# A four-layer graph stack on one core: one PE step split in two, and all engines' orders written anew

## The chip, the cores and the metric

The kernel runs on 1 core of one Trainium2 chip. Times are device microseconds of a whole launch, given as the median of several runs. The profiler adds one execution with every instruction's start and end.

## What is computed

Sixteen graphs of 1024 nodes with 128 features pass through four layers; each adds its result to its input and normalises over the features:

```python
x = _layernorm(x + _L0_gnn_ref(x, adj, W, a))            # one head, additive attention, relu
x = _layernorm(x + _L1_gnn_ref(x, adj, adj, W, a))       # 8 heads of 16, leaky scores, elu
x = _layernorm(x + _L2_gnn_ref(x, adj, rel_w, ...))      # mean over neighbours, linear, norm, relu
x = _layernorm(x + _L3_gnn_ref(x, adj, W))               # 4 heads of 32, dot-product attention
```

`adj` is a 0/1 matrix of 1024 x 1024 for each graph (int32 in memory, about 3% ones).

## The kernel before, in words

One graph is called a batch, b. All tiles of 128 nodes are T = 8. PE is TensorE, DVE VectorE, ACT ScalarE, POOL GpSimd, SP SyncE. Each engine runs one instruction stream, and the streams meet only at semaphores.

**The pipeline.** In a period, four batches are worked on at once: layer 0 and the start of layer 1 for batch n = f+1, the main part of layer 1 for f, layer 2 and layer 3 for k = f-1, and the end of layer 3 for m = f-2. `SECTIONS` lists the periods and `STAGE` says which table serves which: the first three periods have tables of their own (stages 0 to 2), thirteen full periods share one (stage 3), and the last batches have one (stage 4). A table is a dict of step numbers, one number (or list) for a named task, or -1 where the task isn't done; at each step every engine calls the tasks that have this number. So the tables `ON_PE`, `ON_ACT`, `ON_DVE`, `ON_POOL`, `ON_SP` are the order of the work, written out by hand or by a search; they add no wait of their own.

**The tasks that matter here.**

- Layer 0 of batch n: `turn0` (two halves, L895: four transposes each into the same PSUM bank, ACT copies each out to `xfT` before the next), `project0` (three parts, L907, the same bank again, ACT copies `st` and `features` after each), `top0`/`spread0` (L918, L922), `unit0` (eight units, L947: ACT makes a weight tile, L1274, DVE masks it, L1580, PE multiplies, 16 matmuls for one unit).
- Layer 1 of batch f: 64 units in 32 pairs `unit1`: ACT makes two ramps (L1330) from a row spread over all partitions (`s1row`, loaded by SP, L709), or DVE makes them itself (L1660); DVE cuts them with the adjacency (L1674), PE multiplies (L1022, 16 matmuls for a pair). After every four pairs DVE reduces the PSUM (`head1`, L1682). `sum1` (eight tasks, L1003, 24 matmuls each) multiplies the adjacency itself.
- Layer 2 of batch k: `self2` (L1050, L1055), `sum2` (L1069, L1072), and then `turn3`, `project3` (L864, L1088, L1094).
- Layer 3 of batch k: `lengths3`, `maxima3`, `shift3` make a bound for the exponent (DVE L1794 to L1810, PE L1099, L1103); `far` (SP, L754) moves half a tile across partitions by DMA; `scores3` (L1124 for masked ones, L1131), `exp3` (ACT L1378), `masked3` (DVE L1820), `values3` (L1148).
- End of layer 3 of batch m: `turn_back` (L1165): 32 transposes of 33 x 33, in two halves with a semaphore between them; then DVE `finish3` (L1835, L1839), POOL's `residual3`, `stats3`, `tail3`.

**The adjacency's way.** POOL `adjacency` (L831) copies one graph's matrix from int32 to bf16 in DRAM (2048 KB written). SP `adjacency` (L736) issues the DMA transpose into `turned`. POOL `narrow` (L820) copies that to fp8 in `AT`. SP `x` (L699) loads the features of batch n. SP `store_row` and `spread_row` (L717, L721) send a row of layer 0 to DRAM and back to all partitions; DVE `z0` (L1562) and ACT `prepare0` (L1248) wait for it.

The split task, as the kernel before has it, is one function with a wait between its halves:

```python
for x in range(2):
    if x:
        pe.wait_ge(first_turned.sem, first_turned.of(b))
    ...
    last.then_inc((sum3_turned if x else first_turned).sem, 1)
```

## Time and profile before

| | |
|---|---|
| median of 3 runs | 2420.53 us (2417.59 to 2421.40) |
| profiled execution, its own time | 2423.86 us |
| its span, first to last instruction | 2422.1 us |
| PE (matmul) busy | 2242.2 us, 93% |
| DVE busy | 1977.9 us, 82% |
| ACT busy | 1938.1 us, 80% |
| mean granted TensorE clock | 0.969 of full speed |
| DMA | 193.76 MB, 80 GB/s |

How to read it: an engine's busy time is the union of its instructions. Matmuls are pipelined, so a listed matmul is longer than the time that it adds to its group. A clock of 1.00 is 2.4 GHz, and a clock of 0.50 is 1.2 GHz; a stretch with both reads between. Idle time of an engine is put down to what ended it.

### The profile page before, as it was taken

The page shows a single profiled execution, that of the slowest core. Times are in us where ns is not written, and L with a number is a line of the kernel's source. Part 1 is how long each engine was busy: PE and PEld are TensorE (multiplying, and loading weights), DVE is VectorE, ACT ScalarE, POOL GpSimd, SP SyncE. Part 2 cuts the span into 40 slices and gives each one's busy share as a digit, 9 for nine tenths or more (in the row PEclk, how much of TensorE's full clock was granted, in tenths as well). Part 3 has the DMA queues.
Part 4 walks back from the last instruction along what each step waited for, and adds up shares of the span by engine and source line. Part 5 has one row for each costly group of instructions (what it writes and reads, how often), then busy time and mean ns, then how long its engine had stood idle before and what let it go on. Part 6 is the DMA issues. An engine that isn't in the chain of part 4 may idle for free.

```text
span 2422.1 us, 56777 instructions
## 1 busy us (share of the span) xinstructions
PE 2242.2 (93%) x23701; PEld 1528.8 (63%) x23701; DVE 1977.9 (82%) x4206; ACT 1938.1 (80%) x2166; POOL 192.2 (8%) x134
## 2 busy tenths in 40 slices
PE   6667999999999999999999999999999999999977
PEld 5567566585765748576575857658585665857442
DVE  4587788988888898888889888888888889888767
ACT  3858798797988879788787979879797987979735
POOL 0000000001000100100010000001000010010000
PEclk8888999999999999999999999999999999999998
DMA  5625016043251613416062251605225160411100
GB/s 92 159 59 125 19 63 140 28 107 70 70 132 54 141 36 97 80 63 140 29 148 54 69 108 63 140 28 130 63 63 123 61 142 28 106 36 65 34 19 18
DMA packets 190864, 193.76 MB, mean 80 GB/s; under 512 B 129368, under 2 KB 165328, under 8 KB 187728
## 3 DMA queue, kind: packets, MB, share of 16 engines
q1 hardware_dynamic: 183008, 132.99, 20.4%
q0 software_dynamic: 7600, 57.15, 12.1%
q8 instruction: 187, 3.06, 0.5%
q14 instruction: 69, 0.57, 0.1%
HBM read 151.26 MB, written 40.43 MB: 79 GB/s over the span
## 4 chain that ended last, share of the span: by engine, by line
PE 64%; ACT 13%; DVE 11%; issue 7%; DMA 5%; SPq 0%; POOL 0%; ACTq 0%; POOLq 0%; DVEq 0%
PE kp L1148 13%; PE kp L1131 10%; PE fp L1022 9%; PE kp L1003 6%; PE fp L947 6%; ACT ramp L1330 5%; ACT weight L1378 4%; PE kp L1072 4%; PE kp L1124 4%; DVE weight L1580 3%; DMA shared<-shared 2%; PE kp L1069 2%; DVE weight L1820 2%; PE fp L871 2%; PE kp L1165 1%
## 5 line engine op out<-in xcount | busy, mean ns | idle before, releaser
L1330 ACT ACTIVATE ramp<-s1row,tbig 128x1024 fp8e4<-128x1024 f32 x854 | 910.9, 1156 | 12.1 <-DMA s1row<-s_rows_dram 11.9
L1378 ACT ACTIVATE weight<-kp,shift 128x1024 f32<-128x1024 f32 x480 | 511.0, 1112 | 272.1 <-PE kp L1131 266.3
L1148 PE MATMUL kp<-weight,w 128*33 128x512 f32 x1920 | 447.4, 597 | 2.3 <-DVE weight L1820 1.3
L1022 PE MATMUL fp<-vh_parts,weight 128*128 128x102 bf16 x8192 | 418.1, 209 | 30.8 <-issue 11.2
L1022 PEld LDWEIGHTS fp<-vh_parts,weight 128*128 128x128 fp8e4 x8192 | 392.9, 98 | 79.9 <-issue 54.1
L1674 DVE TENSOR_TENSOR weight<-ramp,AT 128x512 int32<-128x512 int32 x512 | 341.7, 687 | 116.3 <-ACT ramp L1330 106.6
L1820 DVE SCALAR_TENSOR_TENSOR weight<-AT,weight 128x1024 f32<-128x1024 fp8e4 x272 | 319.8, 1219 | 46.9 <-ACT weight L1378 46.9
L1131 PE MATMUL kp<-shared 32*128 32x512 f32 x1920 | 274.1, 640 | 23.3 <-ACT weight L1378 23.2
L1148 PEld LDWEIGHTS kp<-weight,w 128*33 128x33 f32 x1920 | 96.7, 110 | 280.2 <-issue 247.9
L947 PEld LDWEIGHTS fp<-features,weight 128*128 128x128 f32 x1840 | 208.8, 192 | 41.1 <-issue 24.4
L1003 PE MATMUL kp<-vh_parts,AT 128*128 128x136 bf16 x3072 | 231.6, 239 | 0.0
L947 PE MATMUL fp<-features,weight 128*128 128x129 f32 x1840 | 217.4, 277 | 5.7 <-DVE weight L1580 5.7
L1003 PEld LDWEIGHTS kp<-vh_parts,AT 128*128 128x128 fp8e4 x3072 | 221.3, 103 | 0.8
L1682 DVE TENSOR_REDUCE vh<-fp 128x272 f32<-128x816 f32 x128 | 128.6, 1005 | 67.5 <-PE fp L1022 66.9
L1131 PEld LDWEIGHTS kp<-shared 32*128 32x128 f32 x1920 | 76.6, 183 | 148.2 <-issue 75.8
L1072 PE MATMUL kp<-elu,AT 128*128 128x128 bf16 x1920 | 170.1, 221 | 0.0
L1069 PE MATMUL kp<-y_hi,AT 128*128 128x129 bf16 x960 | 166.9, 222 | 3.1 <-DVE elu L1734 3.1
L1580 DVE SCALAR_TENSOR_TENSOR weight<-weight,v,AT 128x1024 f32<-128x1024 f32 x123 | 151.8, 1281 | 9.4 <-ACT weight L1274 8.6
L1274 ACT ACTIVATE weight<-xfT,v0neg,v0s 128x1024 f32<-128x1024 f32 x123 | 146.2, 1233 | 13.9 <-PE fp L947 11.9
L1072 PEld LDWEIGHTS kp<-elu,AT 128*128 128x128 fp8e4 x1920 | 149.7, 98 | 0.2
L1124 PE MATMUL kp<-AT,big 128*128 128x512 fp8e4 x480 | 128.0, 382 | 22.1 <-DMA shared<-shared 15.8
L797 POOL TENSOR_TENSOR bsmall<-bsmall,half_neg 128x8 f32<-128x8 f32 x32 | 65.8, 2055 | 878.7 <-DVE bsmall L1480 878.7
(251 smaller groups left out, 2729.8 us busy)
## 6 DMA issues: line engine op xcount, KB each, us to landing
s1row<-s_rows_dram SPq DMA_DIRECT2D x128, 512.0 KB, 4.7
adj_bf_dram<-in_adj_dram POOLq DMA_DIRECT2D x15, 2048.0 KB, 15.2
AT<-turned POOLq DMA_DIRECT2D x15, 1024.0 KB, 9.6
x<-in_x_dram SPq DMA_DIRECT2D x16, 512.0 KB, 6.7
out_dram<-elu SPq DMA_DIRECT2D x16, 512.0 KB, 10.4
xfT<-s_row_dram SPq DMA_DIRECT2D x15, 512.0 KB, 4.5
shared<-shared SPq DMA_DIRECT2D x30, 256.0 KB, 3.7
elu<-x POOLq DMA_DIRECT2D x15, 512.0 KB, 4.6
```

The source lines that it names most:

```text
L947: last = pe.matmul(sums0(b)[:, g, n * (D + 1):(n + 1) * (D + 1)], ring0(b, jt)[:, t * P:(t + 1) * P], h0[:, jt, :], start=(jt == 0 and n = ...
L1003: last = pe.matmul(kp[:, SUM_A_BANKS[t // PER], n * H1 * C1:(n + 1) * H1 * C1].rearrange("p (h c) -> p h c", h=H1), AT[:, third, jt, t * P ...
L1022: last = pe.matmul(fp[:, 1 + t // 4, col:col + 2 * PARTS * C1], edges[:, u % B_RING, t * P:(t + 1) * P], vh_parts[:, jt, h, :, :, :].rearr ...
L1072: last = pe.matmul(sums2(b)[:, g, col:col + D], lhsT, low2(b)[:, jt, k, :], start=False, stop=(jt == T - 1 and k == 1), skip_group_check=True)
L1124: pe.matmul(score_banks(b, w)[:, x, :], big[:], AT[:, third, 2 * J + x, n * HALF:(n + 1) * HALF], start=True, stop=False, skip_group_check ...
L1131: last = pe.matmul(score_banks(b, w)[:, x, :], mine[:, jt * P:(jt + 1) * P], mine[:, n * HALF:(n + 1) * HALF], start=v in masks(b), stop=True,
L1148: last = pe.matmul(kp[side(h), 0, :], values3(b)[:, (2 * J + x) * H3 + h, :], weight3[:, w % P_RING, x * HALF:(x + 1) * HALF], start=(J == ...
L1330: act.activation(ramp[:, u % R_RING, :], s1row[:, h % S_RING, :] if b or h else kp_pair, ACT.Relu, bias=tbig1[:, jt, h:h + 1], scale=BIG, ...
L1378: act.activation(weight3[:, w % P_RING, :], score_banks(b, w).rearrange("p a n -> p (a n)"), ACT.Exp, bias=shifts3(b)[:, h:h + 1], scale=R ...
L1580: dve.scalar_tensor_tensor(out=w, in0=w, scalar=v0[:, jt:jt + 1], in1=AT[:, third, jt, :], op0=ALU.add, op1=ALU.mult).then_inc(weight0_rea ...
L1674: dve.tensor_tensor(edge_words[:, u % B_RING:u % B_RING + 2, :], ramp_words[:, u % R_RING:u % R_RING + 2, :], AT_words[:, third, jt:jt + 2 ...
L1820: dve.scalar_tensor_tensor(out=mine, in0=AT[:, third, 2 * J:2 * J + 2, n * HALF:(n + 1) * HALF], scalar=0.0, in1=mine, op0=ALU.is_equal if ...
```

## The change

1. `layer3_turn_back` becomes two tasks, one for each half, each with a step number of its own. The second half's wait for the first stays. The 32 transposes are the same.
2. Every table has new step numbers, `STEPS` grows from 135 to 138. No table gains or loses any other task. Tiles, rings, semaphores and arithmetic are as before.

```diff
-        STEPS = 135
+        STEPS = 138
...
-            (dict(adjacency=1, narrow=-1, residual3=-1, rstd0=0, rstd1=-1, rstd2=-1, rstd3=-1, rstd_tail=-1),),
-            (dict(adjacency=0, narrow=1, residual3=-1, rstd0=2, rstd1=3, rstd2=-1, rstd3=-1, rstd_tail=-1),),
...
+            (dict(adjacency=0, narrow=-1, residual3=-1, rstd0=1, rstd1=-1, rstd2=-1, rstd3=-1, rstd_tail=-1),),
+            (dict(adjacency=2, narrow=0, residual3=-1, rstd0=1, rstd1=3, rstd2=-1, rstd3=-1, rstd_tail=-1),),
...
-            def layer3_turn_back(b, k):
-
-                pe.wait_ge(sum3_ready.sem, sum3_ready.of(b))
-                if k is not None and k < NB - 1:
-                    pe.wait_ge(sum2_read.sem, sum2_read.of(k))
-                for x in range(2):
-                    if x:
-                        pe.wait_ge(first_turned.sem, first_turned.of(b))
...
+            def layer3_turn_back(b, k, x):
+
+                if x:
+                    pe.wait_ge(first_turned.sem, first_turned.of(b))
+                else:
+                    pe.wait_ge(sum3_ready.sem, sum3_ready.of(b))
+                    if k is not None and k < NB - 1:
+                        pe.wait_ge(sum2_read.sem, sum2_read.of(k))
...
-                if m is not None and s == at["turn_back"]:
-                    layer3_turn_back(m, k)
+                for x in range(2):
+                    if m is not None and s == at["turn_back"][x]:
+                        layer3_turn_back(m, k, x)
```

**PE, a full period, around the turn back.** Before, both halves are one run of 32 (L1165) in the middle of `sum1` (L1003), and the two halves of `turn0` (L895) have other work between them:

```order
L1003 MATMUL kp<-vh_parts,AT 128x136 x48
L895 MATMUL fp<-ident,x 128x128 x4
L1003 MATMUL kp<-vh_parts,AT 128x136 x24
L895 MATMUL fp<-ident,x 128x128 x4
L1022 MATMUL fp<-vh_parts,weight 128x102 x16
L1003 MATMUL kp<-vh_parts,AT 128x136 x24
L1022 MATMUL fp<-vh_parts,weight 128x102 x16
L1165 MATMUL kp<-ident,shared 128x33 x32
L1003 MATMUL kp<-vh_parts,AT 128x136 x96
L1022 MATMUL fp<-vh_parts,weight 128x102 x16
L907 MATMUL fp<-rhs,xfT 128x130 x3
L1022 MATMUL fp<-vh_parts,weight 128x102 x16
```

The same place of the changed kernel:

```order
L1003 MATMUL kp<-vh_parts,AT 128x136 x48
L895 MATMUL fp<-ident,x 128x128 x8
L1022 MATMUL fp<-vh_parts,weight 128x102 x16
L1003 MATMUL kp<-vh_parts,AT 128x136 x24
L907 MATMUL fp<-rhs,xfT 128x130 x3
L1003 MATMUL kp<-vh_parts,AT 128x136 x24
L1165 MATMUL kp<-ident,shared 128x33 x16
L907 MATMUL fp<-rhs,xfT 128x130 x3
L1022 MATMUL fp<-vh_parts,weight 128x102 x16
L1165 MATMUL kp<-ident,shared 128x33 x16
L1003 MATMUL kp<-vh_parts,AT 128x136 x48
L1022 MATMUL fp<-vh_parts,weight 128x102 x16
```

The run of 32 is now two runs of 16 with a part of `project0` and a pair of layer 1 between them; the two halves of `turn0` follow each other directly.

**PE, a full period, at the units of layer 0** (L947, 8 matmuls a unit here), with scores (L1124, L1131) and values (L1148) of layer 3. Before:

```order
L947 MATMUL fp<-features,weight 128x129 x24
L1131 MATMUL kp<-shared 128x512 x4
L947 MATMUL fp<-features,weight 128x129 x16
L1148 MATMUL kp<-weight,w 33x512 x4
L947 MATMUL fp<-features,weight 128x129 x24
L1124 MATMUL kp<-AT,big 128x512 x4
L1131 MATMUL kp<-shared 128x512 x4
L1148 MATMUL kp<-weight,w 33x512 x4
L1131 MATMUL kp<-shared 128x512 x4
```

Now:

```order
L947 MATMUL fp<-features,weight 128x129 x24
L1131 MATMUL kp<-shared 128x512 x4
L947 MATMUL fp<-features,weight 128x129 x40
L1124 MATMUL kp<-AT,big 128x512 x4
L1131 MATMUL kp<-shared 128x512 x4
L1148 MATMUL kp<-weight,w 33x512 x8
L1131 MATMUL kp<-shared 128x512 x4
```

A pair of values (L1148) has moved from between the units to behind the next scores.

**POOL, the first three periods.** The adjacency load (L831), the copy to fp8 (L820) and the small powers of the norms (L797), with what was taken out and put in:

```order
+L831 DMA adj_bf_dram<-in_adj_dram 64x16384
 L797 TENSOR_TENSOR small<-small,half_neg 128x8
-L831 DMA adj_bf_dram<-in_adj_dram 64x16384 x2
 L820 DMA AT<-turned 128x8192
 L797 TENSOR_TENSOR small<-small,half_neg 128x8
+L831 DMA adj_bf_dram<-in_adj_dram 64x16384
 L797 TENSOR_TENSOR fsmall<-fsmall,half_neg 128x8
```

The load for batch 1 comes ahead of the first power, the load for batch 2 moves behind the power of batch 1's layer 0, and in the same way the load for batch 3 (one period on) moves behind that of batch 2's layer 0. On SP the DMA transpose now stands ahead of the load of x in the first periods, and in the full ones ahead of the last two row loads and of `far`, which it followed before.

## Rows read from the trace of the kernel before

**Rows 1.** The page: PE's busy time; granted clock in 40 slices, tenths.
```profile
PE 2242.2 (93%) x23701; PEld 1528.8 (63%) x23701; DVE 1977.9 (82%) x4206; ACT 1938.1 (80%) x2166; POOL 192.2 (8%) x134
...
PEclk8888999999999999999999999999999999999998
```

**Rows 2.** Two full periods: length, PE, PEld, DVE, ACT, POOL busy, PEclk, DMA share, GB/s.
```profile
1617.30:1759.70 142.40, 137.09 (x1481) 92.94 (x1479) 121.73 (x261) 120.82 (x136) 11.97 (x8) 1.00 0.35 87
1759.70:1903.20 143.50, 138.22 (x1481) 94.35 (x1479) 121.74 (x261) 120.62 (x136) 11.96 (x8) 0.99 0.36 86
```

**Rows 3.** The chain that ended last: start, length; one step of three periods.
```profile
904.29 5.28 PE kp L1148 x24
...
1046.35 5.28 PE kp L1148 x24
...
1189.87 5.28 PE kp L1148 x24
```

**Rows 4.** Stretches at and behind the turn back, in two periods (columns as Rows 2).
```profile
1081.26:1083.67 2.41, 2.35 (x35) 2.20 (x34) 2.34 (x6) 2.41 (x4) 0.00 (x0) 1.00 0.00 0
1083.67:1088.00 4.33, 4.33 (x46) 4.33 (x46) 4.26 (x11) 0.34 (x1) 0.00 (x0) 0.61 0.01 4
...
1655.91:1658.32 2.41, 2.35 (x35) 2.20 (x34) 2.34 (x6) 2.41 (x3) 0.00 (x0) 1.00 0.03 7
1658.32:1662.60 4.28, 4.28 (x68) 4.28 (x68) 4.21 (x11) 1.58 (x4) 0.00 (x0) 1.00 0.00 0
```

**Rows 5.** PE timeline right behind the turn back, in the same two periods.
```profile
1083.60 7.89 PE L1003 MATMUL kp<-vh_parts,AT 128*128 128x136 bf16 x96
...
1658.26 6.46 PE L1003 MATMUL kp<-vh_parts,AT 128*128 128x136 bf16 x96
```

**Rows 6.** PE, ACT and SP timeline of one full period, with PE's waits in brackets.
```profile
1792.32 0.60 PE L895 MATMUL fp<-ident,x 128*128 128x128 f32 x4
...
1793.36 0.61 ACT L1235 ACTIVATE xfT<-fp 128x512 f32<-128x512 f32 x1
...
1810.94 0.94 PE L907 MATMUL fp<-rhs,xfT 128*128 128x130 f32 x6 [0.65 <-ACT features L1235]
...
1820.79 0.27 PE L1099 MATMUL kp<-ident,qmax 128*4 128x128 f32 x1 [0.98 <-DVE qmax L1798]
...
1824.31 1.02 PE L1124 MATMUL kp<-AT,big 128*128 128x512 fp8e4 x4 [1.27 <-DMA shared<-shared]
...
1876.01 1.14 PE L1131 MATMUL kp<-shared 32*128 32x512 f32 x8 [0.52 <-ACT weight L1378]
...
1884.38 1.14 PE L1131 MATMUL kp<-shared 32*128 32x512 f32 x8 [0.44 <-ACT weight L1378]
...
1820.44 10.58 SPq L736 DMA_TRANSPOSE turned<-adj_bf_dram  x1
```

**Rows 7.** The page: DMA issues, KB each, median us to landing.
```profile
s1row<-s_rows_dram SPq DMA_DIRECT2D x128, 512.0 KB, 4.7
adj_bf_dram<-in_adj_dram POOLq DMA_DIRECT2D x15, 2048.0 KB, 15.2
```

**Rows 8.** The second period: POOL's load, the chain's store, DVE's wait, ACT's early ramps.
```profile
85.56 0.52 POOL L831 DMA_DIRECT2D adj_bf_dram<-in_adj_dram  x1 [36.91 <-DMA turned<-adj_bf_dram]
...
90.52 9.39 DMA s_row_dram<-row
...
107.05 0.75 DVE L1562 TENSOR_SCALAR xfT<-xfT,T 128x1024 f32<-128x1024 f32 x1 [6.88 <-DMA xfT<-s_row_dram]
...
59.27 4.13 ACT L1330 ACTIVATE ramp<-kp,tbig 128x1024 fp8e4<-128x1024 f32 x4 [0.33 <-PE kp L970]
```

**Rows 9.** The third period: POOL's load, then the waits of DVE and PE.
```profile
218.87 0.56 POOL L831 DMA_DIRECT2D adj_bf_dram<-in_adj_dram  x1
...
234.99 1.42 DVE L1660 TENSOR_SCALAR ramp<-s1row,st 128x1024 fp8e4<-128x1024 f32 x2 [9.90 <-DMA s1row<-s_rows_dram]
...
237.55 2.88 PE L1022 MATMUL fp<-vh_parts,weight 128*128 128x102 bf16 x32 [9.03 <-issue]
```

More of the change, by code:

```diff
@@ new lines, in graph_stack @@
+            (dict(cut1=[83, 87], cut1_second=[93, 95], elu=58, exp3=[31, 32, 36, 37, 42, 43, 48, 49, 52, 53, 55, 56,
+                 59, 61, 63, 64, 65, 66, 68, 69, 71, 72, 74, 75, 77, 78, 80, 81, 84, 85, 90, 91], exps0=41, exps1=79,
+                 first2=88, out3=[62, 67, 86, 96], prepare0=44, project0=[17, 18, 22], project1=73, project3=26,
+                 ramps=[1, 2, -1, 3, 4, 5, -1, 6, 7, 8, 10, 11, 12, 15, 16, 19, 20, 25, 28, -1, 29, 30, -1, 33, 34,
+                 -1, 35, 38, 39, 40], ramps_ahead=[89, 94], second2=92, self2=0, sources1=76, sum1=[13, 23, 24],
+                 turn0=[9, 14], turn1=70, turn2=82, turn3=21, unit0=[45, 46, 47, 50, 51, 54, 57, 60], wide3=27),),
@@ new lines, in graph_stack @@
+            (dict(cut1=[84, 88], cut1_second=[89, 93], elu=63, exp3=[32, 33, 35, 36, 39, 40, 43, 44, 47, 49, 54, 55,
+                 58, 59, 62, 64, 65, 66, 68, 69, 71, 72, 74, 75, 77, 78, 82, 83, 86, 87, 90, 91], exps0=37, exps1=79,
+                 first2=85, out3=[48, 67, 81, 96], prepare0=46, project0=[16, 21, 23], project1=73, project3=27,
+                 ramps=[0, 1, -1, 2, 3, 4, -1, 5, 6, 8, 9, 10, 11, 14, 15, 17, 20, 22, 26, -1, 29, 30, -1, 31, 34, -1,
+                 38, 41, 42, 45], ramps_ahead=[92, 95], second2=94, self2=7, sources1=76, sum1=[18, 19, 24],
+                 turn0=[12, 13], turn1=70, turn2=80, turn3=25, unit0=[50, 51, 52, 53, 56, 57, 60, 61], wide3=28),),
@@ new lines, in graph_stack @@
+            (dict(affine2=19, columns1=[80, 81], cut1=[86, 88], cut1_third=[89, 90], divide1=65, elu1=73, finish0=70,
+                 finish1=61, finish3=-1, head1=[10, 16, 22, 26, 36, 45, 51, 57], lengths3=31, low2=87, masked3=[-1,
+                 -1, -1, -1, 66, -1, 69, -1, 72, -1, 74, 79, 82, 83, 84, -1], maxima1=77, maxima3=32, maximum0=48,
+                 most0=42, norm0=71, norm1=75, norm3=25, out2=8, ramps=[-1, -1, -1, -1, 1, -1, -1, -1, 6, -1, -1, -1,
+                 -1, -1, -1, -1, -1, -1, -1, -1, -1, 37, -1, -1, 40, -1, -1, 46, -1, -1, -1, -1], relu2=24, rest2=85,
+                 shift0=56, shift3=35, shifts1=78, stats2=12, stats3=-1, tail3=-1, top0=28, top1=76, unit0=[58, 59,
+                 60, 62, 63, 64, 67, 68], unit1=[0, 2, 3, 4, 5, 7, 9, 11, 13, 14, 15, 17, 18, 20, 21, 23, 27, 29, 30,
+                 33, 34, 38, 39, 41, 43, 44, 47, 49, 50, 53, 54, 55], z0=52),),
@@ new lines, in graph_stack @@
+            (dict(affine2=22, columns1=[83, 84], cut1=[86, 89], cut1_third=[92, 93], divide1=72, elu1=76, finish0=73,
+                 finish1=65, finish3=25, head1=[6, 11, 21, 32, 41, 48, 55, 61], lengths3=35, low2=91, masked3=[-1, -1,
+                 -1, -1, 60, -1, 69, -1, 74, -1, 77, 81, 85, 87, 88, -1], maxima1=79, maxima3=36, maximum0=45,
+                 most0=40, norm0=75, norm1=80, norm3=26, out2=15, ramps=[-1, -1, -1, -1, 2, -1, -1, -1, 10, -1, -1,
+                 -1, -1, -1, -1, -1, -1, -1, -1, -1, -1, 33, -1, -1, 43, -1, -1, 47, -1, -1, -1, -1], relu2=23,
+                 rest2=90, shift0=51, shift3=39, shifts1=82, stats2=17, stats3=46, tail3=58, top0=27, top1=78,
+                 unit0=[62, 63, 64, 66, 67, 68, 70, 71], unit1=[0, 1, 3, 4, 5, 7, 8, 9, 12, 13, 14, 16, 18, 19, 20,
+                 24, 28, 29, 30, 31, 34, 37, 38, 42, 44, 49, 50, 52, 53, 56, 57, 59], z0=54),),
```

214 lines of the change are left out of this document (93 added, 121 removed).

## The prediction

> **What bounds the kernel.** I read the page first, then the stretches by period, then the chain of waits, then the timelines of PE, ACT and DVE through one full period and through the first three. PE is busy 93% of the span [rows 1]: it sets the time, and a change of order can only win back what PE idles and what it does at the lower clock. In a full period of 143.50 us PE is busy 138.22, so 5.3 us are idle; DVE and ACT are busy about 122 and 121 us, each with some 20 us to spare [rows 2]. Thirteen full periods make most of the run. The same step of the chain comes 142.06 us later once and 143.52 us later the next time [rows 3]. The short period is the one whose clock reads 1.00; of the 13 full ones, 11 read 0.99 and 2 read 1.00, as in the two shown [rows 2].
>
> The difference sits in one place. While PE turns back layer 3's sums, it is busy 2.35 of 2.41 us, but with blocks of 33 x 33. Right behind it the granted clock is 0.61 over 4.33 us in the one period, so part of it at 0.50, and 1.00 in the other [rows 4]. The 96 matmuls that follow take 7.89 us there and 6.46 us here [rows 5]: a fall costs 1.43 us, and the chain says the same (143.52 - 142.06 = 1.46).
>
> The first three periods are another matter: there PE waits for transfers. In the second, DVE waits 6.88 us for a row that went to DRAM and back; its first leg alone took 9.39 us for a 4 KB row, with the adjacency load of batch 2 issued 5 us before [rows 8]. In the third, DVE waits 9.90 us and PE 9.03 us for a row load that was issued within half a microsecond of the adjacency load of batch 3 [rows 9]. Such a row load lands in 4.7 us as a rule, the adjacency load in 15.2 [rows 7].
>
> **The change, part by part.** The sum is made against the profiled execution's own 2423.86 us. That is 3.3 us above the median of the runs shown, so the median goes down with it and stays some 3 us lower.
>
> *The split turn back.* It removes the one wait of PE on itself and adds no instruction. Both runs of 16 transposes are about 1.2 us long (half of 2.41), with six matmuls of `project0` (0.94 us [rows 6]) and the 16 of a layer 1 pair between them (1.1 us at most, at the 67 ns a matmul of [rows 5]), which is dense work. If the fall comes from a long run of such small blocks, it doesn't come from half of one. There are 12 falls behind this step (11 full periods and the one after them). I take all twelve away: 12 x 1.43 = **-17 us**. The bounds are 0 (each fall stays, or comes elsewhere) and -17.
>
> Here the Trainium skill speaks against the change. TensorE: Matmul & The Clock Gate, Part 1, has the clock halved when the engine has been idle, and released by activity. By that rule a stretch that is busy 2.35 of 2.41 us is no cause, and splitting it would win nothing. The trace disagrees with so plain a reading, since the fall comes behind this step in 11 of 13 periods, with no wait ahead of it; but what counts as activity no row here shows.
>
> *The adjacency load of batch 3, third period.* It moves behind the power of batch 2's layer 0, which comes at the end of that period. Then the row load of 219 us meets nothing of that size. The stall shrinks from 15.6 us of transfer to the usual 4.7 [rows 7], which is 10.9, and DVE stood 9.90 and PE 9.03 for it. The copy to fp8 now goes out between the two powers of layer 2, ahead of the row load, and should be mostly done. I take **-10 us**, between -4 (the rows still meet the copy) and -11. Who is late next: PE's own work, dense from there on.
>
> *The adjacency load of batch 2, second period.* It too leaves the row's way. The row should be back in some 7 us after the store's issue instead of 16.5. But the new order pays first: ACT makes its four early ramps, 4.13 us [rows 8], behind the first cuts of layer 1's columns instead of while it waits, so layer 1 starts 4 to 5 us later; x of batch 1 is loaded behind the transpose's issue. I follow the ACT stream, which is busy nearly throughout: some 5 us later at the start, 7 us of waiting gone, and near the period's end `norm0` and PE's next transposes come ahead of `finish1` and `divide1`, which DVE did first. Sum **-4 us**, bounds +3 (only the loss) and -9 (only the gains).
>
> *The full period's order, clock aside.* I walked the new PE order with the measured durations.
> - The two halves of `turn0` now follow each other. The second needs ACT's copy of the first: 0.61 us and two semaphores, about 0.9 us idle where other matmuls stood before [rows 6]. In return the wait of 0.65 us in `project0` is covered by the split halves.
> - `lengths3` on DVE now stands behind two ramps and a cut. PE's wait for it grows from 0.98 to about 1.5 us. The wait for `far`, 1.27 us [rows 6], takes most of that back: scores begin about 0.2 us later, counted from the same start.
> - At layer 0's units five in a row need the masks one by one, about 0.6 us of new waiting; the waits of 0.52 and 0.44 us [rows 6] go, since the exponentials are asked for earlier and `elu` no longer stands before one of them. Later `sources1` and `maxima1` stand ahead of the scores, which gives part of it back.
> - At the period's end ACT makes two ramps ahead of a cut and `second2`: layer 2's sums may wait 0.2 us.
>
> The items are +0.25, +0.2, -1.0 and +0.2 or so, **-0.4 us** a period, 13 x 0.4 = **-5 us**. Each is uncertain by as much as itself, so the bounds are +8 and -13. The transpose's issue on SP (10.58 us [rows 6]) now stands ahead of two row loads instead of behind `far`; those wait for edges that DVE makes later anyway, so I price it at nothing. If that cover fails, the ramps of layer 1 wait.
>
> *The ends.* Layer 3's last batches are ordered nearly as before: 0.
>
> *New falls.* With the period no longer 143.5 us, PE's waits around `maxima3` (two of about 1 us with little between) can lead to a fall in some periods. I count two: **+3 us**.
>
> Sum: -17 - 10 - 4 - 5 + 3 = -33. 2423.9 - 33 = 2391 profiled, and 3 less for the median: **2388 us**.
>
> **The rivals.**
>
> *A: the fall stays, or moves.* Either the skill's rule is right, and the small blocks are no cause, or the new order's thinner places (`turn0` with its wait, 1.5 us at `maxima3`) bring one fall in each period. The time is 2388 + 17 - 3 = 2402 where it stays everywhere. For it: both places are thinner than before. Against: the idle places of before (0.98 and 1.27 us within 4 us) never led to a fall. Chance 0.18.
>
> *B: the transfers meet again.* The loads still stall the first periods, by the copy to fp8 or the transpose. Then 14 us of gain go: 2402. Against it: the queue's order puts them 10 us apart. Chance 0.10.
>
> *C: slower.* In each period `lengths3` stands behind a ramp pair (1.42 us) and a cut, and behind it hang PE's L1099, the shift, all scores and all exponentials. If DVE comes there 2.9 us or more later than I reckon, PE has no pairs left to cover it: 13 x 2.9 = 38 us, and the median is 2426 or more. It decides from 2.9 us a period on: (33 + 5) / 13, the gain and what a measurement can tell. Against: DVE has 20 us to spare in a period, and `top0` waits for ACT for at most a microsecond. Chance 0.04.
>
> *D: no effect.* Both costs that the order avoids are replaced by others of the same size: 2420. Chance 0.05.
>
> **How the numbers follow.** Forecast 0.63, A 0.18, B 0.10, D 0.05, C 0.04. About 0.2% (5 us) is what a measurement of this kernel tells from no change. Forecast, A and B lie beyond it on the fast side: faster 0.91; D is the same, with a little of C: same 0.05; slower 0.04. The range takes the bounds of the orders (-13 and +8 around -5) and reaches up past A and B: 2374 to 2408.
>
> **What would show it.** In the profile after: full periods of about 141.7 us, all with a clock of 1.00 or nearly all; 96 or 48 matmuls of L1003 behind L1165 at 67 ns apart; no wait of 10 us for `s1row` near 219 us, and none of 7 us on `xfT` near 107; PE's idle time per period 4.5 to 5.3 us with about 0.9 us at L895 and 1.5 us at L1099. I am wrong if full periods still read 0.99, if PE's waits in a period exceed 6 us, or if DVE and PE still stand for 9 us or more in the third period.

## The result, and the profile after

The changed kernel takes 2385.64 us (median of 4 runs, 2385.24 to 2386.31), the kernel before 2420.13 us beside it (2417.59 to 2421.40, 4 runs): the ratio is 0.9859, 95% interval 0.9842 to 0.9876. The profiled execution has a span of 2383.9 us where the one before had 2422.1, so 38.2 us have to be found.

The page of the changed kernel, beside [rows 1] and [rows 7]:

```profile
PE 2219.4 (93%) x23701; PEld 1497.8 (63%) x23701; DVE 1970.3 (83%) x4206; ACT 1943.8 (82%) x2166; POOL 197.6 (8%) x134
...
PEclk8889999999999999999999999999999999999989
...
s1row<-s_rows_dram SPq DMA_DIRECT2D x128, 512.0 KB, 4.0
adj_bf_dram<-in_adj_dram POOLq DMA_DIRECT2D x15, 2048.0 KB, 13.0
```

PE has the same 23701 matmuls and is busy 22.8 us less, by the clock that it runs at. Its idle time went down by the other 15.4 us.

Two full periods of the changed kernel (columns as in [rows 2]: length, busy time of PE, PEld, DVE, ACT and POOL, granted clock, DMA share, GB/s), and the stretches at the turn back of one of them, beside [rows 4]: first half, what stands between, second half, what follows.

```profile
1025.82:1167.28 141.46, 137.12 (x1481) 92.68 (x1480) 121.11 (x260) 121.08 (x136) 12.45 (x8) 1.00 0.36 87
1591.68:1733.15 141.47, 137.12 (x1482) 92.69 (x1480) 121.12 (x260) 121.08 (x137) 12.45 (x8) 1.00 0.37 87
...
1060.45:1061.63 1.18, 1.18 (x19) 1.14 (x17) 1.15 (x6) 1.18 (x4) 0.00 (x0) 1.00 1.28 290
1061.63:1063.15 1.52, 1.52 (x24) 1.43 (x23) 1.44 (x11) 1.52 (x3) 0.00 (x0) 1.00 0.21 45
1063.15:1064.33 1.18, 1.18 (x19) 1.14 (x18) 0.77 (x2) 1.18 (x4) 0.91 (x1) 1.00 0.00 0
1064.33:1068.66 4.33, 4.33 (x69) 4.33 (x70) 3.78 (x14) 4.31 (x6) 2.07 (x2) 1.00 0.53 151
```

Every full period now has a clock of 1.00, the full 2.4 GHz; the stretch behind the turn back reads 1.00 where [rows 4] has 0.61. The chain's step L1148 x24, beside [rows 3], comes every 141.47 us, with none of the jumps of before:

```profile
1020.61 5.28 PE kp L1148 x24
...
1162.08 5.27 PE kp L1148 x24
...
1303.54 5.28 PE kp L1148 x24
```

A full period held 5.28 us of idle PE before and holds 4.34 now. PE's timeline of one, its rows with a wait, beside [rows 6]:

```profile
1055.29 0.66 PE L895 MATMUL fp<-ident,x 128*128 128x128 f32 x4 [0.69 <-ACT xfT L1236]
...
1064.26 3.31 PE L1003 MATMUL kp<-vh_parts,AT 128*128 128x136 bf16 x48
...
1077.43 0.27 PE L1099 MATMUL kp<-ident,qmax 128*4 128x128 f32 x1 [1.32 <-DVE qmax L1799]
1080.11 0.38 PE L922 MATMUL fp<-tmost,ones 1*128 1x1 f32 x2 [0.55 <-DVE tmost L1549]
```

The new waits are there (0.69 us in `turn0`, 1.32 at L1099), and one of 0.55 at L922 (`spread0`) that I hadn't foreseen. The wait of 1.27 us for the far rows and that of 0.65 in `project0` are gone; of the three for the exponentials (0.52, 0.44 and 0.38 us) two of 0.38 and 0.20 are left. The 48 matmuls of L1003 behind the second half take 3.31 us, 69 ns each.

POOL's timeline of the first periods shows the adjacency loads of batches 2 and 3, beside [rows 8] and [rows 9]; under it the stretch up to the third period, and the third period, in the changed kernel:

```profile
143.01 0.56 POOL L831 DMA_DIRECT2D adj_bf_dram<-in_adj_dram  x1
...
283.94 0.56 POOL L831 DMA_DIRECT2D adj_bf_dram<-in_adj_dram  x1
...
0.00:171.19 171.19, 108.43 (x1178) 96.41 (x1178) 111.62 (x236) 103.73 (x130) 9.79 (x15) 0.86 0.49 112
171.19:318.58 147.39, 136.71 (x1449) 92.46 (x1447) 116.97 (x233) 125.80 (x140) 8.05 (x6) 0.99 0.25 67
```

and in the kernel before:

```profile
0.00:176.68 176.68, 114.55 (x1178) 104.49 (x1179) 111.48 (x236) 103.62 (x130) 9.37 (x15) 0.83 0.44 99
176.68:335.34 158.66, 140.81 (x1449) 95.07 (x1446) 117.23 (x232) 125.50 (x140) 9.37 (x6) 0.94 0.30 73
```

The loads went out at 143.01 and 283.94 us instead of 85.56 and 218.87, and in neither of these two periods does DVE wait for a DMA any more. (PE still waits 0.9 us for the far rows in the third.) The third period is 11.3 us shorter, the part ahead of it 5.5.

The one place that got slower is the end. The stretch from the last batch's layer 2 sums to the last instruction, before and after:

```profile
2302.30:2422.10 119.80, 93.72 (x657) 37.38 (x653) 82.02 (x170) 51.79 (x53) 10.22 (x5) 0.89 0.07 18
```

```profile
2260.65:2383.90 123.25, 96.60 (x671) 38.19 (x669) 82.42 (x170) 55.89 (x57) 10.22 (x5) 0.87 0.07 18
```

So the 38.2 us are: 5.5 + 11.3 in the first three periods, 24.3 in the 13 full ones (143.33 us each on average before, 141.46 after), 0.6 in the stretch behind them (103.67 and 103.10 us), less 3.4 at the end.

### The profile page after: what moved, and what is told of

It is laid out like the page before. It is cut to its first block, busy times and chain, and to the rows that moved or that the text cites. A ratio compares the mean times of both kernels' runs of the same rounds, so it can differ in the third digit from the quotient of the medians.

```text
span 2383.9 us, 56775 instructions
## 1 busy us (share of the span) xinstructions
PE 2219.4 (93%) x23701; PEld 1497.8 (63%) x23701; DVE 1970.3 (83%) x4206; ACT 1943.8 (82%) x2166; POOL 197.6 (8%) x134
## 4 chain that ended last, share of the span: by engine, by line
PE 64%; DVE 19%; ACT 8%; issue 7%; DMA 1%; POOL 0%; SPq 0%; POOLq 0%; DVEq 0%; ACTq 0%
PE kp L1148 14%; PE fp L1022 10%; PE kp L1131 10%; PE kp L1003 7%; DVE weight L1581 5%; PE kp L1072 4%; PE kp L1124 4%; ACT weight L1379 4%; PE fp L947 3%; DVE weight L1675 2%; DVE weight L1821 2%; PE kp L1069 2%; ACT ramp L1331 2%; PE fp L864 1%; PE fp L871 1%
## 5 line engine op out<-in xcount | busy, mean ns | idle before, releaser
L1148 PE MATMUL kp<-weight,w 128*33 128x512 f32 x1920 | 447.5, 599 | 7.5 <-DVE weight L1821 7.5
L1022 PE MATMUL fp<-vh_parts,weight 128*128 128x102 bf16 x8192 | 412.5, 208 | 28.3 <-DVE weight L1675 17.6
L1022 PEld LDWEIGHTS fp<-vh_parts,weight 128*128 128x128 fp8e4 x8192 | 386.0, 97 | 82.2 <-DVE weight L1675 50.2
L1675 DVE TENSOR_TENSOR weight<-ramp,AT 128x512 int32<-128x512 int32 x512 | 334.2, 685 | 70.6 <-ACT ramp L1331 63.1
L1148 PEld LDWEIGHTS kp<-weight,w 128*33 128x33 f32 x1920 | 97.0, 110 | 314.0 <-issue 252.7
L1131 PE MATMUL kp<-shared 32*128 32x512 f32 x1920 | 273.7, 639 | 10.2 <-ACT weight L1379 10.2
L947 PEld LDWEIGHTS fp<-features,weight 128*128 128x128 f32 x1840 | 209.0, 192 | 36.9 <-DVE weight L1581 23.3
L947 PE MATMUL fp<-features,weight 128*128 128x129 f32 x1840 | 217.8, 278 | 9.0 <-DVE weight L1581 9.0
L1003 PE MATMUL kp<-vh_parts,AT 128*128 128x136 bf16 x3072 | 215.4, 228 | 1.7 <-ACT vh_rest L1236 1.1
L1003 PEld LDWEIGHTS kp<-vh_parts,AT 128*128 128x128 fp8e4 x3072 | 203.6, 97 | 2.8 <-ACT vh_rest L1236 1.3
L1131 PEld LDWEIGHTS kp<-shared 32*128 32x128 f32 x1920 | 75.9, 183 | 112.7 <-issue 69.5
L797 POOL TENSOR_TENSOR bsmall<-bsmall,half_neg 128x8 f32<-128x8 f32 x32 | 65.0, 2030 | 911.8 <-DVE bsmall L1481 911.8
L1124 PE MATMUL kp<-AT,big 128*128 128x512 fp8e4 x480 | 127.4, 380 | 2.8 <-ACT weight L1379 0.9
```

The costliest lines, as they stand in the source:

```text
L947: last = pe.matmul(sums0(b)[:, g, n * (D + 1):(n + 1) * (D + 1)], ring0(b, jt)[:, t * P:(t + 1) * P], h0[:, jt, :], start=(jt == 0 and n = ...
L1003: last = pe.matmul(kp[:, SUM_A_BANKS[t // PER], n * H1 * C1:(n + 1) * H1 * C1].rearrange("p (h c) -> p h c", h=H1), AT[:, third, jt, t * P ...
L1022: last = pe.matmul(fp[:, 1 + t // 4, col:col + 2 * PARTS * C1], edges[:, u % B_RING, t * P:(t + 1) * P], vh_parts[:, jt, h, :, :, :].rearr ...
L1124: pe.matmul(score_banks(b, w)[:, x, :], big[:], AT[:, third, 2 * J + x, n * HALF:(n + 1) * HALF], start=True, stop=False, skip_group_check ...
L1131: last = pe.matmul(score_banks(b, w)[:, x, :], mine[:, jt * P:(jt + 1) * P], mine[:, n * HALF:(n + 1) * HALF], start=v in masks(b), stop=True,
L1148: last = pe.matmul(kp[side(h), 0, :], values3(b)[:, (2 * J + x) * H3 + h, :], weight3[:, w % P_RING, x * HALF:(x + 1) * HALF], start=(J == ...
```

## The experiments

Each kernel was timed against the kernel before on its own chip, where that one read 2422.7 to 2427.5 us as a median; so ratios are compared first. "Falls" counts the full periods of the traced execution in which the granted clock falls at or right behind the turn back; in a period in which it does, the stretch behind reads 0.6 instead of 1.00. The mean period and the falls are those of one execution of each kernel, the median is that of all.

| kernel | median us | ratio to before | mean full period | falls, of 13 |
|---|---|---|---|---|
| before | 2420.1 | 1 | 143.33 | 11 |
| changed | 2385.6 | 0.9859 (0.9842 to 0.9876) | 141.46 | 0 |
| joined | 2403.9 | 0.9904 (0.9876 to 0.9931) | 142.81 | 11 |
| split | 2403.3 | 0.9909 (0.9876 to 0.9943) | 141.69 | 0 |
| early | 2405.6 | 0.9917 (0.9891 to 0.9943) | 143.09 | 7 |
| tail | 2383.6 | 0.9827 (0.9801 to 0.9853) | 141.47 | 0 |
| twice | 2421.9 | 0.9989 (0.9975 to 1.0004) | 143.45 | 0 |
| dense | 2422.8 | 0.9999 (0.9989 to 1.0008) | 143.71 | 0 |
| loads | 2403.2 | 0.9922 (0.9907 to 0.9937) | 143.21 | 8 |
| last | 2392.4 | 0.9878 (0.9863 to 0.9894) | 141.48 | 0 |
| jdense | 2427.8 | 1.0016 (1.0006 to 1.0025) | 144.08 | 3 |
| quad | 2456.5 | 1.0135 (1.0116 to 1.0153) | 146.37 | 13 |
| best | 2384.6 | 0.9846 (0.9830 to 0.9861) | 141.47 | 0 |
| both | 2382.8 | 0.9817 (0.9798 to 0.9836) | 141.49 | 0 |

### Is it the split? joined and split

joined, from the changed kernel, in the full periods:

```diff
-turn_back=[31, 34]
+turn_back=[31, 31]
```

> The changed kernel with one number changed back in its full periods: both halves of the turn back stand at one place again (where the first half stands now), all else as changed. Theory S (a run of 32 small blocks lets the clock fall, two runs of 16 do not): the clock is granted at half rate for a few us behind the turn back in most of the 13 full periods, the 96 matmuls of L1003 or what stands there take 1.4 us more, a full period takes 142.5 to 142.9 instead of 141.46 us, and the time is 2386 + 13 to 19 = 2399 to 2405 us. Theory O (the falls went because the period is shorter and other work moved, the split is bystander): no fall comes back, the full periods stay at 141.5 us, 2385 to 2387 us.

split, from the kernel before (whose one place is 28), in the full periods:

```diff
-turn_back=[28, 28]
+turn_back=[28, 31]
```

> The kernel before with the split alone: in the full periods the second half of the turn back stands three tasks behind the first, with layer 1 sums and a pair between them; every other table is as before. Theory S: no fall behind L1165 in the full periods, 11 to 12 falls of 1.43 us less, full periods of 142.0 to 142.4 us, the time 2420 - 14 to 17 = 2403 to 2406 us. Theory O: falls in 9 or more of 13 periods remain, 2416 to 2421 us. The stalls of the second and third period are unchanged by both.

One number brings the falls back: 11 of 13, and the time to 2403.9. One number takes them all away from the kernel before, in the traced execution: 2403.3 us as a median. That execution was the fastest of its four (2399.06 us, mean granted clock 0.978); the other three took 2400.5 to 2406.1 us with 0.974 and 0.975, so PE was longer at the lower clock in them, and where is not on record. The changed kernel's four all read 0.983 or 0.984. Two full periods of joined, with the run of small blocks and the stretch behind it in such a period each, the first with a fall and the second without (same columns):

```profile
749.33:892.38 143.05, 138.62 (x1482) 94.18 (x1480) 121.04 (x260) 121.11 (x137) 12.44 (x8) 0.99 0.37 86
1035.36:1176.88 141.52, 137.10 (x1481) 92.68 (x1480) 121.06 (x260) 121.10 (x136) 12.44 (x8) 1.00 0.37 87
927.01:929.43 2.42, 2.36 (x35) 2.21 (x33) 2.32 (x13) 2.42 (x5) 0.00 (x0) 1.00 0.64 145
929.43:933.80 4.37, 4.37 (x46) 4.36 (x47) 4.30 (x18) 4.37 (x8) 2.98 (x2) 0.63 0.33 122
1070.00:1072.42 2.42, 2.36 (x35) 2.21 (x33) 2.32 (x13) 2.42 (x5) 0.00 (x0) 1.00 1.27 290
1072.42:1076.80 4.38, 4.38 (x68) 4.37 (x69) 4.31 (x18) 4.38 (x8) 2.98 (x2) 1.00 0.59 188
```

A fall costs 1.53 us in this order (143.05 - 141.52), all of it busy time: 46 matmuls where 68 fit. With joined also the part of the order alone can be read: 142.81 - 143.33 = -0.52 us a period at the same number of falls. The split alone gives 141.69 - 143.33 = -1.64, both together -1.87. The parts come to more than the whole, and each of them alone already takes away the wait of 0.65 us in `project0`; that would also be why split's period is 0.3 us and more shorter than the 142.0 to 142.4 us that I expected. Theory S holds, theory O falls.

### What makes the fall: twice, dense, jdense, quad

Joined has two periods without a fall though PE's run in them is the same to the hundredth (2.36 busy of 2.42 us). So the run isn't all of it. twice, from the changed kernel (halves apart, each done twice):

```diff
-                for g in range(len(GROUPS)):
+                for g in [g for _ in range(2) for g in range(len(GROUPS))]:
```

> The changed kernel with every transpose of the turn back issued twice (32 + 32 instead of 16 + 16 small blocks, the second time over the first, the output unchanged); the halves still stand at two places. It adds 32 x 74 ns = 2.4 us of small blocks to each of 16 turn backs. If a run of small blocks as long as the joined one lets the clock fall: falls within 1.1 us of the end of one or both halves in most of the 13 full periods, 13 x 2.4 plus 11 to 20 x 1.5 on top of the changed kernel: full periods of 145 to 147 us, 2440 to 2460 us. If the fall came from the engine's wait between the joined halves (0.06 us) or from the place, and not from the length: no falls, full periods of 143.9 us, 2415 to 2426 us.

dense, its control, from the changed kernel:

```diff
+                if not x:
+                    for g in [g for _ in range(5) for g in range(len(GROUPS))]:
+                        for n, t in enumerate(GROUPS[g]):
+                            pe.matmul(kp[:, g, n * H3 * C3:n * H3 * C3 + P], big[:], big[:], start=True, stop=True)
```

> The control to the kernel with doubled transposes: the changed kernel with 40 matmuls of 128 x 128 in bf16, some 2.3 us of dense work, issued ahead of the first half of each turn back into the space that the transposes then write (output unchanged). As much time and delay for the rest as the doubled small blocks, but no small blocks. Small-block theory: no fall in the full periods, 143.7 to 144.1 us each, 2415 to 2426 us. If what counts is that the period gets longer or the work behind is pushed to other moments: falls in most full periods, as with the doubled transposes, 2435 us or more.

I missed twice: two runs of 32 blocks a period, 2.17 us each and 1.52 apart, and no fall in any of the 13 periods traced. Added time alone makes none either (dense). (The trace of twice is that of its fastest execution, 2417.39 us; the nine others took 2417.99 to 2423.29.) One period of twice, its two runs and what stands between and behind:

```profile
1034.59:1178.06 143.47, 139.12 (x1514) 94.69 (x1512) 121.17 (x260) 121.08 (x137) 12.45 (x8) 1.00 0.35 86
1069.23:1071.40 2.17, 2.17 (x35) 2.13 (x33) 2.10 (x11) 2.17 (x5) 0.00 (x0) 1.00 0.85 191
1071.40:1072.92 1.52, 1.52 (x23) 1.42 (x23) 1.27 (x8) 1.52 (x4) 0.71 (x1) 1.00 0.00 0
1072.92:1075.10 2.18, 2.18 (x35) 2.14 (x34) 0.00 (x0) 2.18 (x4) 1.32 (x1) 1.00 0.59 203
1075.10:1079.40 4.30, 4.30 (x68) 4.30 (x69) 3.79 (x14) 2.31 (x3) 0.96 (x1) 1.00 0.23 53
```

That sent me back to the times of the falls. In joined, the clock falls this long after the end of the run, period by period: -0.03, 0.21, 0.48, 0.78, 1.10 us, none, -0.10, 0.17, 0.44, 0.74, 1.08, none, -0.12. It slides by some 0.3 us a period up to 1.1, then a period goes by without one, is 1.5 us shorter, and it begins anew. In the kernel before the 11 falls lie between -0.02 and 1.01 us from the run's end too. So a second theory: the run costs only where its end meets the chip's own moment, and a period of about 143.1 us with its fall happens to come back to that moment again and again. jdense and quad test it. jdense is joined with the four added lines of dense; quad is joined with the edit of twice, so one run of 64 blocks.

> The changed kernel with both halves of the turn back at one place in the full periods (as in the joined kernel, which had a fall behind 11 of 13) and 40 bf16 matmuls of 128 x 128, 2.3 us of dense work, ahead of the first half. The run of 32 small blocks is the same, the period is 2.3 us longer, so its run ends at another moment, seen from the fall before. Theory M (a fall needs the run and the right moment; in the kernels with 143.1 us the period itself keeps bringing the run to the right moment): falls behind 2 to 6 of 13 full periods, mean full period 143.9 to 144.5 us, 2425 to 2432 us. Theory R (the run alone decides): falls behind 11 to 13, mean full period 145.1 us, 2436 to 2440 us.

> The changed kernel with both halves at one place in the full periods and every transpose issued twice: one run of 64 small blocks, 4.4 us. Theory M: a run of twice the length meets the right moment in every period, wherever it stands: a fall at or within the run or within 1.1 us of its end in 12 or 13 of 13 full periods, and the small blocks inside it run at the lower clock, 1 to 2 us each time: mean full period 145 to 146.5 us, 2435 to 2455 us. Rival L (small blocks are no cause, only the place between its neighbours in the joined kernel was): few falls, mean full period 143.5 us, 2415 to 2424 us.

jdense: the same run of 32 blocks, the period 2.2 us longer (143.75 against 141.52, without a fall), and only 3 falls in 13 (0.86, 0.83 and 0.81 us behind the run's end). quad: a fall in 13 of 13, 2.2 to 3.9 us from the start of the run. Periods with and without a fall of jdense, and the stretches behind their runs:

```profile
1037.64:1182.89 145.25, 140.83 (x1521) 96.42 (x1520) 121.16 (x260) 121.12 (x137) 12.44 (x8) 0.99 0.37 85
1182.89:1326.63 143.74, 139.33 (x1522) 94.91 (x1520) 121.15 (x260) 121.12 (x137) 12.44 (x8) 1.00 0.33 86
1076.93:1081.30 4.37, 4.37 (x45) 4.36 (x45) 3.79 (x14) 3.55 (x5) 1.30 (x2) 0.61 0.47 151
1222.18:1226.50 4.32, 4.32 (x67) 4.31 (x68) 3.78 (x14) 3.54 (x5) 1.31 (x2) 1.00 0.46 148
```

A full period of quad, and one of its runs, whose last part already goes at the lower clock:

```profile
1050.87:1197.36 146.49, 142.08 (x1513) 97.60 (x1512) 121.16 (x260) 121.17 (x137) 12.45 (x8) 0.98 0.34 84
1085.51:1090.36 4.85, 4.79 (x66) 4.62 (x65) 3.36 (x17) 4.85 (x9) 1.88 (x1) 0.88 0.27 71
```

So a long run at one place does it (joined and quad against the changed kernel and dense), and the moment decides whether a run of 32 pays (3 of 13 against 11 of 13). quad's time, 2456.5 us, is 1.5 over what I gave it. Runs of 16 blocks never had a fall behind them in a full period: in the changed kernel, split, tail, last, dense, best and both that is 7 x 13 x 2 = 182 runs, in periods of 141.3 to 143.7 us, so ending at many different moments. For twice the moment is only argued: its runs end 143.47 us apart, the falls of joined come 143.36 apart, so a run that missed the moment once went on missing it. I didn't run twice at another period.

What it is about the run stays open. Its blocks are small, they are transposes in f32, and in the middle of it PE waits 0.06 us, the second half for the first. Every kernel with falls at the turn back (before, joined, early, loads, jdense, quad) has that wait inside the run; twice has runs of 32 without it, and no fall. For twice I had written no falls and 2415 to 2426 us in case this wait or the place is the cause and not the length, and so it came (2421.9); neither jdense nor quad, which both keep the wait, tells this apart from the moment. Nor does any run put large transposes, or small blocks that are no transposes, in its place. Shown is that dividing the run ends the falls.

The Trainium skill, TensorE: Matmul & The Clock Gate, Part 1, says that the monitor behind the clock runs on its own and doesn't start anew with the kernel, so that the place of the first change depends on the moment at which the work meets it. The falls here are later ones, but they agree: 11, 3 and 13 of them for one run, the same run at another period, and a run of twice the length.

### The first periods: early and loads

early has the changed order of the first three stages on all engines and the kernel before from there on.

> The kernel before with the changed order of the first three stages (before the first full period) on all engines; full periods and the end as before. If the gains of the first periods are their own: the first full period starts 16 to 18 us earlier (5.5 up to the third period, 11.3 in it), the full periods keep 143.3 us with falls in about 11 of them, and the time is 2402 to 2405 us. If instead they only shift waiting into the first full period: 2410 us or more.

The third period took 147.38 us and the full ones began at 318.7, 16.6 us earlier: as expected. But 13 of the same full periods, entered at another moment, had 7 falls behind the turn back instead of 11: 143.09 us on average. Its last stage gave part of that back (105.27 us up to the last batch instead of 103.67), and the time is 2405.6.

It also has a fall that has nothing to do with the turn back: one at the idle places, 23 us behind it, in a period of 144.46 us. PE's two waits there, and the stretch from 515.92 us on (columns as before):

```profile
511.70 0.27 PE L1122 MATMUL kp<-ident,qmax 128*4 128x128 f32 x1 [0.98 <-DVE qmax L1822]
...
516.03 1.87 PE L1147 MATMUL kp<-AT,big 128*128 128x512 fp8e4 x4 [2.09 <-DMA shared<-shared]
...
515.92:519.34 3.42, 3.31 (x12) 0.95 (x12) 2.41 (x4) 0.75 (x1) 0.00 (x0) 0.50 1.25 257
```

The kernel before waits 0.98 us and then 0.77 to 1.58 us at the same two places, without a fall in 13 periods. Here the wait for the far rows was 2.09 us. In one period of loads, below, it was 1.57 us and the clock fell at its end too, while 1.77 us in another period of loads had no fall. So a wait can bring a fall as a run can, not every time either, and the changed order, which has no wait for the far rows in its full periods, took this risk away with it.

loads takes from the change only POOL's order in the first three stages:

```diff
-(dict(adjacency=1, narrow=-1, ..., rstd0=0, ...),),
-(dict(adjacency=0, narrow=1, ..., rstd0=2, rstd1=3, ...),),
-(dict(adjacency=3, narrow=0, ..., rstd0=4, rstd1=5, rstd2=1, ...),),
+(dict(adjacency=0, narrow=-1, ..., rstd0=1, ...),),
+(dict(adjacency=2, narrow=0, ..., rstd0=1, rstd1=3, ...),),
+(dict(adjacency=4, narrow=1, ..., rstd0=3, rstd1=5, rstd2=0, ...),),
```

> The kernel before with POOL's order alone changed in the first three stages: the adjacency load of the batch after next stands behind the power of layer 0 (batch 2's and 3's load go out 10 us or more later), the narrow copy ahead of it. All other engines as before. Theory T (the rows waited for meeting transfers): the third period shrinks from 158.7 to 147 to 149 us, nearly the whole 11.3 us, and up to its start 3 to 6 us go; 2420 - 11 to 17 = 2403 to 2409 us. Theory O (the gain needs the other engines' order too, ramps and the copies): the third period stays above 153 us, 2413 us or more.

Its first part, its third period, and POOL's load of batch 3's adjacency:

```profile
0.00:169.45 169.45, 113.14 (x1178) 103.27 (x1179) 111.48 (x236) 103.55 (x130) 9.46 (x15) 0.82 0.46 103
169.45:315.62 146.17, 136.66 (x1450) 92.17 (x1447) 117.09 (x232) 125.66 (x140) 9.33 (x6) 0.99 0.31 79
...
280.30 0.56 POOL L854 DMA_DIRECT2D adj_bf_dram<-in_adj_dram  x1
```

POOL's few lines alone give the whole gain, more than I expected (147 to 149 us), and 1.2 us more in the third period than the change (146.17 against 147.39; best and both, with the same tables, have 146.17 and 146.20). The other engines' new order there costs those 1.2 us; which part of it does isn't shown. The first part says less: with the changed tables it lasted from 169.9 to 172.9 us in nine kernels, so 169.45 isn't apart from them (best and both, with POOL's order alone, have 172.1 and 171.4); the two kernels with the old tables, before and split, have 176.7 and 175.7.

### The end: tail, last, best, both

tail is the changed kernel with the last stage wholly as before.

> The changed kernel with the order of the last stage (last two batches of layer 3) as before. The stretch from the last batch's layer 2 sums to the end took 123.25 us after the change and 119.8 before. If the last stage's order is the cause: 119.5 to 120.5 us there again and a time of 2382 to 2384 us. If it is the state in which the last period is entered (the clock, what stands in the queues): 123 us and 2385 to 2387 us.

The last batch takes what it did before, but the stretch ahead of it is 2.3 us longer than in the changed kernel:

```profile
2156.32:2261.69 105.37, 98.10 (x1199) 68.21 (x1198) 84.52 (x189) 88.62 (x90) 8.30 (x5) 0.98 0.14 42
2261.69:2381.40 119.71, 93.57 (x657) 37.39 (x653) 82.00 (x170) 51.80 (x53) 10.22 (x5) 0.89 0.07 18
```

So the last stage's order does cause the loss at the end. Ahead of it this stage has the run of 32 again with a fall behind it, and PE waits 1.7 us at the turn of layer 2's x where the kernel before had 0.2. Together the two stretches take 225.1 us here, 226.4 in the changed kernel and 223.5 before. last tried to have both, with the two scores of the batch ahead taken out of the last batch's layer 2 sums and put in front (ACT's exponentials 20 and on to match, and the last batch's own tables as before):

```diff
-scores3=[..., 74, 78, 83, 88, ...], self2=76, sum2=[77, 79, 80, 81, 82, 84, 85, 86]
+scores3=[..., 74, 76, 77, 87, ...], self2=77, sum2=[78, 79, 80, 81, 82, 83, 84, 85]
```

> The changed kernel with the order of the last batch alone as before (its layer 2 sums to the end: two scores and three exponentials of the batch ahead stand where they stood before); the rest of the last stage, with its split turn back, as changed. Theory: the loss of 3.4 us at the end comes from the last batch's order, where units done early leave one wait of 5.1 us behind them and a fall of 6.8 us, and the earlier part of that stage is as good as in the changed kernel: 103.1 us up to the last batch, 119.7 us from there, 2382 us. Rival: the units left over are missing in the stretch before, which then waits: 104.5 us or more, and 2384 us or more.

It failed: ahead of the sums PE stood 2.07 and 2.33 us for the exponentials, the clock was low for 10.2 us from the end of the first of them on, and the two stretches take 111.4 and 121.1 us. The rival holds.

best took another guess at the end, and loads' order at the start:

```diff
-values3=[..., 95, 96, 97], turn3=98           # PE
+values3=[..., 95, 96, 98], turn3=97
-masked3=[..., 69, 70, 73, -1], affine2=71, relu2=72   # DVE
+masked3=[..., 69, 72, 73, -1], affine2=70, relu2=71
-out3=[..., 72], turn3=73                      # ACT
+out3=[..., 73], turn3=72
```

> A candidate: full periods as changed; in the first three stages only POOL as changed, the other engines as before (the run with the loads alone began its full periods at 315.6 us against 318.6 in the changed kernel); and in the last stage, as changed, the turn of x of the last batch stands ahead of the last unit of the batch before it, on DVE affine2 and relu2 ahead of a mask, on ACT the turned copy ahead of the last sums' copy, all three as in the kernel before. If both hold: full periods from 315.6 us on at 141.5 us, the last batch in 119.7 to 121 us instead of 123.25, 2379 to 2382 us. If the last stage's loss comes from the scores done early and not from this: 122.5 to 123.5 us there and 2382 to 2384 us. If the gain of the loads is lost beside the new full period: 2385 us or more.

The last batch takes 124.25 us: the guess was wrong. Its full periods began at 318.3 us and not at 315.6, since its first part took 172.1. What is left is in the timelines. PE of the changed kernel in the last batch, where two scores (1.14 us each) stand among the layer 2 sums, then the end of its work:

```profile
2264.32 1.14 PE L1131 MATMUL kp<-shared 32*128 32x512 f32 x8
...
2270.92 1.14 PE L1131 MATMUL kp<-shared 32*128 32x512 f32 x8
...
2297.00 5.55 PE L1148 MATMUL kp<-weight,w 128*33 128x512 f32 x16 [5.09 <-DVE weight L1821]
```

and DVE's norm of layer 2 of that batch, which every later step of it waits for, in the changed kernel and before:

```profile
2279.03 1.65 DVE L1469 BATCH_NORM_STATS2 bstat<-yb 128x6 f32<-128x128 f32 x8
```

```profile
2318.32 1.65 DVE L1468 BATCH_NORM_STATS2 bstat<-yb 128x6 f32<-128x128 f32 x8
```

The norm begins 18.4 us after the stretch does (2279.03 - 2260.65), 16.0 before (2318.32 - 2302.30): the two scores lie on the one chain that is left at the end. By my reading the work that they bring forward is missing later, so PE stands once for 5.09 us, where the kernel before had six waits of 0.4 to 2.4 us; the clock is low behind it, and 16 matmuls of L1148 take 5.55 us, where they took 3.63 in the kernel before. 2.4 + 1.9 = 4.3 us, of which 3.4 stay. Shown is that the stage's order costs it (tail); that the two scores do is argued from these lines, since last and best each changed other things too.

both combines what was measured: full periods as changed, POOL's loads alone in the first stages, the last stage as before.

> The last candidate: full periods as changed; in the first three stages only POOL as changed, the other engines as before; the whole last stage as before. By the pieces measured so far: third period 146.2 us, 13 full periods of 141.48 us (no fall, since the split stays), up to the last batch 105.4 us, the last batch 119.7 us. Span 2380 to 2382 us with a first part of 169.5 to 172 us, time 2381 to 2384 us, 2 to 4 us under the changed kernel's 2385.6. Rival: the pieces are not additive (the start of the full periods moves with the first part's own spread, or a fall enters a full period): 2385 us or more.

```profile
2156.91:2262.11 105.20, 98.19 (x1199) 67.08 (x1198) 84.48 (x189) 88.44 (x90) 8.30 (x5) 0.98 0.15 42
2262.11:2383.40 121.29, 96.56 (x657) 37.86 (x653) 82.04 (x170) 51.83 (x53) 10.22 (x5) 0.86 0.07 18
```

2382.8 us, as forecast, but its last batch took 121.29 us and not 119.7, with the same instructions. PE is busy 3.0 us more in it than in tail (96.56 and 93.57): behind a wait that tail and the kernel before have as well, at 2.4 us, without a fall, the clock fell here.

```profile
2280.61 2.01 PE L1154 MATMUL kp<-shared 32*128 32x512 f32 x8 [2.36 <-ACT weight L1402]
```

The eight matmuls of that row take 2.01 us, 1.14 at the full clock. This traced execution is also the slowest of its five (2385.12; the others 2380.8 to 2382.8). both is the fastest kernel here by its median; its interval (0.9798 to 0.9836) lies just below that of the change (0.9842 to 0.9876), yet the runs beside which they stand differ by 6 us, so I'd call the 2.8 us likely and not shown.

## Why the prediction was right, step by step

I said 2388 us, and the time is 2385.6. The sum was -33 us on the profiled execution, and 38.2 came. Of those 5 us, 3 were made good by luck: I took the median to stay 3 us under the profiled execution, and after the change the two are equal (2385.64 and 2385.68). By its terms:

- **The split turn back, -17.** The mechanism holds in that the run of 32 brings the fall and its halves apart don't; what about the run does it is open, its small blocks or something else. The falls cost less in the full periods: those without a fall were 142.20 us long before (two), those with one 143.53 (eleven), so 11 x 1.33 = 14.7 us; with the twelfth, the stretch went only from 103.67 to 103.10, 0.6. But the split as an edit is worth more than its falls: split took 1.64 us off a period, 21 us in thirteen, since the halves' new places also cover the 0.65 us wait in `project0`, which I had booked under the order. And the rule was incomplete: I took the run's length as the whole cause. It needs the moment too (jdense, and early with 7 falls for the same tables), so "12" was a count that held for one start of the period only.
- **Rival A, the rule against it.** That idleness alone halves the clock is refuted by the rows: falls come behind a run that is busy 2.36 of 2.42 us, and not behind the waits of 0.69 and 1.32 us in the changed period. No full period of the changed kernel has a fall. The Trainium skill, TensorE: Matmul & The Clock Gate, Part 1, has the clock halved when the engine has been idle; that nothing else does it was my reading. On idleness the traces agree: falls came at the end of waits of 2.09 us (early) and 1.57 us (loads). I had held against rival A that the idle places never led to a fall; that was true of one trace only.
- **The third period, -10: -11.3.** My reason was POOL's load, and POOL alone does it (loads). DVE waits for no row load there any more; a wait of PE for the far rows, 0.9 us, is left.
- **The second period, -4: -5.5** up to the third period, of which I can tell the sign but, by the spread of 169.9 to 172.9 us, not the parts. The cost that I had given the later ramps isn't seen apart; the other engines' new order costs 1.2 us, in the third period.
- **The full period's order, -0.4 a period.** The waits came out nearly as walked: 0.69 us for `turn0` (I said 0.9), 1.32 for `lengths3` (1.5), those of `project0` and `far` gone. At the masks I had 0.6 us of new waiting, and it is some 0.2 at layer 0's units (0.30 and 0.23 against 0.36) and 0.2 at a value; one of 0.55 came at `spread0`, where I had none. Idle PE per period fell by 0.94 us (5.28 to 4.34), and against periods without a fall the gain is 142.20 - 141.46 = 0.74, 9.6 us in all where I had 5. Most of that the split alone gives too: on top of it the order adds 141.69 - 141.46 = 0.23 us a period, 3 us in all.
- **New falls, +3: none.** The places that I feared had none in 13 periods, with waits of 1.32 and 0.55 us.
- **The ends, 0: +3.4.** This is the step that was wrong in kind. I called the last batches "ordered nearly as before" and didn't follow the two scores that moved into the last batch's sums. There PE is busy only 96.6 of 123.3 us and isn't the bound any more; a chain of DVE, ACT and PE is, and the norm on it began 2.4 us later.

The sum of what was measured is -14.7 - 0.6 - 9.6 - 16.8 + 3.4 = -38.3. So the total is better than its terms: the split's falls came out 1.7 us smaller than forecast, the order 4.6 larger, and the missing new falls (3) and the unforeseen loss at the end (3.4) cancelled each other; the first periods gave 2.8 more than forecast.

## What to carry to other kernels

Where PE is the bound, look at the granted clock period by period and not on average: a place that costs a fall in most periods and none in a few may be a run of small blocks whose end comes back to the same moment. Here cutting such a run in two with dense work between ended the falls in all seven traces, in periods of 141.3 to 143.7 us (what the slower, untraced executions of split did is open). Move a big load away from a row that someone waits for before touching any other engine's order: here three lines on POOL gave all of that gain. A wait of PE can bring a fall of its own, in one period and not in the next. And read a last batch by itself, as a chain: work that is free in a full period lies on the path there.

## What I had not expected of the chip

- For the same run of 32 small blocks the clock fell in 11, 7 or 8 of 13 periods (before, early, loads) in kernels whose full periods have the same tables and start at other moments, and in 11 or 3 (joined, jdense) in two whose periods differ by 40 added matmuls. All 25 falls of before, joined and jdense began between 0.12 us ahead of the run's end and 1.10 us behind it.
- 40 dense matmuls of 128 x 128 and 32 transposes of 33 x 33 cost a period nearly the same (143.72 and 143.47 us against 141.46), though the dense ones are full blocks: 56 ns for a dense one, 63 for a small one.
- A wait of PE can be harmless in one kernel and bring a fall in another that has the same instructions there: the one of 2.36 us in the last batch did in both and not in tail.
- The first 170 us of a launch vary by 3 us between nine kernels whose instructions there are the same (169.9 to 172.9), where the 13 full periods of the changed kernel differ by 0.24 us at most (141.29 to 141.53).
